# The feed-forward path of a two-layer cross-attention kernel, taken a slot sooner and its first product split around the scores

## What is computed

```python
# layer 0, per batch
qkv  = ln(x, g1, be1) @ w_qkv + b_qkv
ckv  = context @ w_ckv + b_ckv
attn = softmax(mask(q @ concat(k_self, k_ctx).T / sqrt(8)))      # causal over own tokens
x    = x + attn @ concat(v_self, v_ctx)
hdn  = ln(ln(x, g2, be2), gf, bf) @ w1 + b1                      # 128 -> 512
x    = x + gelu(hdn) @ w2 + b2                                   # 512 -> 128
# layer 1, per batch
Q, K, V = ln(x, ln_w, ln_b) @ wq.T + bq, context @ wk.T + bk, context @ wv.T + bv
out  = softmax(key_mask(Q @ K.T / sqrt(8))) @ V @ wo.T + bo + x
```

## Time and profile before

| | |
|---|---|
| median of 3 runs | 465.14 us (463.82 to 467.96) |
| the profiled execution | 466.13 us, its span 463.7 us, mean granted TensorE clock 0.915 |
| PE busy | 384.7 us (83%), 8885 matmuls |
| DVE busy | 295.5 us (64%) |
| ACT busy | 262.5 us (57%) |
| POOL busy | 139.8 us (30%) |
| chain of waits, by engine | PE 50%, DVE 18%, issue 9%, ACT 8%, DMA 8%, POOL 4% |

### The profile page before, as it was taken

The page is one execution under the profiler, slowest core; times in us unless marked ns, Lnnn a source line. Parts: engine busy times, 40 slices in busy tenths (PEclk is TensorE's granted clock), DMA queues, the critical chain, the costliest instruction groups (busy, mean ns, idle before and its releaser), DMA issues.

```text
span 463.7 us, 20194 instructions
## 1 busy us (share of the span) xinstructions
PE 384.7 (83%) x8885; PEld 278.6 (60%) x8885; DVE 295.5 (64%) x738; ACT 262.5 (57%) x459; POOL 139.8 (30%) x207
## 2 busy tenths in 40 slices
PE   3668879996989799988899798979898989686766
PEld 1346657564666576657576567667676676453654
DVE  5426786469568774796658675796389459706232
ACT  2567635763756476464846386556656756343451
POOL 7100533046205520363105520461047106302000
PEclk9957986999999899998999899998999999877586
DMA  6755164115342542153404542253201400121101
GB/s 192 198 151 123 54 171 140 34 56 137 108 119 93 121 147 59 69 129 111 134 3 146 106 131 60 94 122 122 60 26 43 125 3 26 58 82 47 48 4 45
DMA packets 41974, 42.86 MB, mean 92 GB/s; under 512 B 3208, under 2 KB 34392, under 8 KB 41888
## 3 DMA queue, kind: packets, MB, share of 16 engines
q1 hardware_dynamic: 40436, 39.86, 31.2%
q0 software_dynamic: 624, 1.26, 1.0%
q10 hardware_dynamic: 828, 0.46, 0.3%
HBM read 23.65 MB, written 17.83 MB: 89 GB/s over the span
## 4 chain that ended last, share of the span: by engine, by line
PE 50%; DVE 18%; issue 9%; ACT 8%; DMA 8%; POOL 4%; SPq 1%; ACTq 1%; DVEq 0%; POOLq 0%
PE dense L689 12%; PE dense L712 7%; DVE top L1011 5%; PE key L845 3%; PE mixed L875 3%; PE mixed L883 3%; DMA k_stack<-scratch_k 3%; PE key L836 3%; PE side L908 3%; PE dense L694 3%; PE dense L702 2%; PE query L795 2%; PE query L803 2%; DVE k_part L1001 2%; ACT probs L523 2%
## 5 line engine op out<-in xcount | busy, mean ns | idle before, releaser
L1011 DVE TENSOR_REDUCE top<-query 128x8 f32<-128x1024 f32 (+1 forms) x96 | 117.2, 1220 | 70.9 <-PE query L803 54.7
L523 ACT ACTIVATE probs<-key 128x1024 f32<-128x1024 f32 x96 | 98.4, 1025 | 81.9 <-PE key L845 55.7
L462 POOL TENSOR_TENSOR top<-top 128x8 bf16<-128x8 f32 (+1 forms) x96 | 20.3, 213 | 207.2 <-DVE top L1011 206.5
L845 PE MATMUL key<-top_row,spread 48*64 48x128 bf16 x1536 | 48.7, 226 | 3.8 <-ACT top_row L528 3.6
L455 POOL TENSOR_TENSOR rstd_x<-var_eps_x,half 128x4 f32<-128x4 f32 x24 | 24.5, 1020 | 71.6 <-DVE var_eps_x L973 71.6
L544 ACT COPY o_t<-mixed 128x256 f32<-128x256 f32 x96 | 35.3, 368 | 13.4 <-PE mixed L896 7.8
L875 PE MATMUL mixed<-probs,v 128*32 128x128 f32 x1024 | 41.7, 281 | 0.0
L836 PE MATMUL key<-q_stack,k_stack 48*64 48x128 f16 x1024 | 40.1, 221 | 0.0
L689 PE MATMUL dense<-normed_ft,w 128*128 128x512 f32 x64 | 34.2, 663 | 5.1 <-ACT normed_ft L564 5.1
L845 PEld LDWEIGHTS key<-top_row,spread 48*64 48x64 bf16 x1536 | 33.8, 109 | 6.1 <-ACT probs L523 4.9
L908 PE MATMUL side<-cst,o_t 128*128 128x128 f32 x192 | 34.1, 304 | 0.7 <-ACT mix_t L551 0.7
(11 more groups left out here) (120 smaller groups left out, 782.1 us busy)
## 6 DMA issues: line engine op xcount, KB each, us to landing
k_stack<-scratch_k SPq DMA_DIRECT2D x16, 384.0 KB, 6.2
q_stack<-scratch_q SPq DMA_DIRECT2D x64, 96.0 KB
scratch_k<-k_part SPq DMA_DIRECT2D x8, 512.0 KB, 2.8
scratch_k<-k_part SPq DMA_DIRECT2D x16, 256.0 KB, 2.6
scratch_q<-q_part SPq DMA_DIRECT2D x16, 256.0 KB, 2.7
k_stack<-scratch_k SPq DMA_DIRECT2D x16, 192.0 KB
x_in<-in_x SPq DMA_DIRECT2D x8, 256.0 KB, 3.2
scratch_q<-q_part SPq DMA_DIRECT2D x16, 128.0 KB, 2.4
```

The source lines that it names most:

```text
L523: nc.scalar.activation(probs[u.number % 2][:].rearrange("p h q -> p (h q)"), key[:].rearrange("p h x -> p (h x)"), ACT.Exp, scale=SCALE).t ...
L845: ins = nc.tensor.matmul(key[T * n:T * n + T, h, a * P:(a + 1) * P], spread[u.layer][rows, A2 * h + a, T * n:T * n + T], top_row[u.number ...
L1011: nc.vector.tensor_reduce(maxima, query[:].rearrange("p h x -> p (h x)").rearrange("p (a k) -> p a k", a=w), AX_X, ALU.max, negate=True).t ...
```

## The change

The second norm's statistics and root come in slot 10 instead of 11, its rows in slot 11 instead of 12, `f_t` in slot 12 instead of 13. The products with w1 keep their slots (13 and 14), but leave `dense` and `dense_first` for a function of their own, `up`, which PE runs between `by_query` and `by_key`. The GELUs of `w1_0` and `w1_1` stay at the end of ACT's slot 13; those of `w1_2` and `w1_3` are written at the head of slot 14, ahead of the exponential. The one-column GELU is left for the last chunk alone.

```diff
-JOBS = (("f_t", L0, 13), ("w1_0", L0, 13), ...
+JOBS = (("f_t", L0, 12), ("w1_0", L0, 13), ...
...
         @block.gpsimd
-                for c in due(11, s):
+                for c in due(10, s):
                     root(c, "x1_again")
...
         @block.scalar
+            def gelu(c, f):
+                nc.scalar.activation(hidden[:, f, :], job(f"w1_{f}", c)[:], ACT.Gelu,
+                                     bias=cols[:, B1 + f:B1 + f + 1]).then_inc(s_read[f"w1_{f}"], 1)
...
-                for c in job_due("w1_1", s):
+                for c in job_due("w1_0", s):
                     if c > 0:
                         act.wait_ge(s_done["w2b"], c)
-
-                    act.wait_ge(s_half, 1)
-                    nc.scalar.activation(unread[:, c:c + 1], half[:, 0:1], ACT.Gelu)
-                    for f in range(FC):
-                        nc.scalar.activation(hidden[:, f, :], job(f"w1_{f}", c)[:], ACT.Gelu,
-                                             bias=cols[:, B1 + f:B1 + f + 1]).then_inc(s_read[f"w1_{f}"], 1)
+                    if c == LAST:
+
+                        act.wait_ge(s_half, 1)
+                        nc.scalar.activation(unread[:], half[:, 0:1], ACT.Gelu)
+                    gelu(c, 0)
+                    gelu(c, 1)
...
             for s in ALL:
+                for c in job_due("w1_2", s):
+                    gelu(c, 2)
+                    gelu(c, 3)
                 if s + 1 in UNIT:
                     exp(UNIT[s + 1])
...
         @block.tensor
                 for c in job_due("f_t", s):
                     pe.wait_ge(s_norm["x1_again"], c + 1)
                     transposes("f_t", c, normed_f)
+
+            def up(s):
+                for c in job_due("w1_0", s):
+                    pe.wait_ge(s_read["f_t"], c + 1)
+                    product("w1_0", c, w1[:, 0:P], normed_ft)
+                    product("w1_1", c, w1[:, P:2 * P], normed_ft)
                 for c in job_due("w1_2", s):
                     product("w1_2", c, w1[:, 2 * P:3 * P], normed_ft)
                     product("w1_3", c, w1[:, 3 * P:4 * P], normed_ft)
...
-                for c in job_due("w1_0", s):
-                    pe.wait_ge(s_read["f_t"], c + 1)
-                    product("w1_0", c, w1[:, 0:P], normed_ft)
-                    product("w1_1", c, w1[:, P:2 * P], normed_ft)
...
                 if s + 3 in UNIT:
                     by_query(UNIT[s + 3])
+
+                up(s)
                 if s + 1 in UNIT:
                     by_key(UNIT[s + 1])
...
         @block.vector
-                for c in due(12, s):
+                for c in due(11, s):
                     norm_rows(c, "x1_again", normed_f, normed_f)
...
-                for c in due(11, s):
+                for c in due(10, s):
                     dve.wait_ge(s_offset, c + 1)
                     stats("x1_again", normed_f, range(TILES))
```

More of the change, by code:

```diff
@@ L84, in last_unit @@
     return max(u.number for u in UNIT.values() if (u.layer, u.chunk) == (layer, c))
-JOBS = (("f_t", L0, 13), ("w1_0", L0, 13), ("w1_1", L0, 13), ("w1_2", L0, 14), ("w1_3", L0, 14), ("ctx_t", IN, -22),
+JOBS = (("f_t", L0, 12), ("w1_0", L0, 13), ("w1_1", L0, 13), ("w1_2", L0, 14), ("w1_3", L0, 14), ("ctx_t", IN, -22),
         ("w2a", L0, 15), ("k_ctx", IN, -21), ("w2b", L0, 16), ("x_t", IN, -20), ("k0", IN, -19), ("out", L1, 9), ("out_a", OUT_A, 0),
@@ L176, in xattn_program @@
         half = sb("half", [P, TILES])
-        unread = sb("unread", [P, CHUNKS])
+        unread = sb("unread", [P, 1])
         cst = sb("cst", [P, CW])
```

## The result

| | before | the change |
|---|---|---|
| median of 4 runs each | 464.48 us (462.40 to 467.96) | 476.77 us (472.28 to 479.60) |
| ratio, with its interval | | 1.0225 (1.0117 to 1.0332) |
| profiled execution | 466.13 us, span 463.7 us, clock 0.915 | 472.28 us, span 470.4 us, clock 0.918 |
| PE / DVE / ACT busy | 384.7 / 295.5 / 262.5 us | 386.2 / 296.3 / 261.9 us |

The change makes the kernel slower by 12.3 us in the medians; 476.5 was forecast. The ratios in this document are taken over the fast runs alone, without the slow ones (here that of 479.60 us), and so differ a little from the ratio of the medians.

What follows compares the result with a forecast made beforehand. PE, busy 83% of the span and holding half the chain of waits, was taken to bound the kernel. 466.1 + 8.4 (stall less gains) + 3.1 (clock) = 477.6, as a median 476.5; range 468.5 to 483.5.

Steps and rivals of the forecast that it cites:

- The stall: Slot 14, chunks 0 to 6: PE idles 2.44 us ahead of the third product with w1, until the first GELU ends.
- The gains: Per chunk, PE's wait for the scaled `f_t` goes (0.55 us); its wait behind slot 14's exponential shrinks by 0.66.
- The clock in half of the chunks: Behind the idle stretch in slot 14 the clock falls in half of the chunks, 1.26 us each, 4.4 in all.
- rival of a fall in every chunk: The clock falls behind slot 14's idle stretch in all seven chunks: 8.8 us on top of 8.4, 482.3; chance 0.15.
- the one without a fall: Rival: PE's idle stretch in slot 14 costs its 8.4 us and the clock nothing, 473.5; chance 0.2.
- One fall spared: Of four clock falls behind PE's waits without a releaser, chunks 2 to 5, one may go: -1.3 us.
- faster rival: The four waits without a releaser and their falls vanish: at most 15 us back against 8.4, 458.5; chance 0.07.
- The table load: ACT's load ahead of the first GELU costs 1.28 us; with the skill's added drain the stall would be 3.8.
- Chunk 1: PE's wait of 1.22 us ahead of `ctx_t` takes up some 0.3, so this chunk loses 0.9 instead of 1.2.
- Start and tail: Ends of the kernel: only chunk 7 changes, its transposes moving beside ACT's scaling, 0 to 0.5 us, taken as 0.2.
- The distance of the chunks: Sign: first products of chunks 2, 3 and 4 move from 51 us apart to 52.3 or more.
- rival of a loss taken up: A DMA or DVE chain binds behind slot 15 and absorbs half the loss: +4.2, 468.3 as a median; chance 0.1.

Runs made afterwards that it cites:

- half of the change: The change with the third and fourth products with w1 put back behind the scores by key of slot 14; 475.25 us against 462.80, ratio 1.0245.
- the pair of kernels with the stall open and filled: The change, 476.94 us, beside the change with two more overwritten products of 128x512 in PE's idle stretch, 469.56 us; ratios 1.0402 and 1.0217.

## Why the prediction was right

- **The stall** (2.44 predicted): 2.48 or 2.49 in each of chunks 0 to 6, in every profile of the change. The path was to be 12.27 and is 12.40; before 11.05. Shown as cause by three kernels: undoing the first pair's move takes it down to 0.80, half of the change keeps the distance of 6.34, and 0.50 more on ACT makes it 2.99.
- **The gains** (0.55 and 0.66): the first is there. PE does not wait for the scaled `f_t`; alone this brought 5.1 us, with an interval that takes in the 3.9 predicted. The second is only a shift. The wait behind the exponential went from 1.01 to 0.23 (0.35 predicted), but the 5.09 us from the third product to the scores by key of slot 15 are the same before, in the change and with only the first half moved. The prediction subtracts 0.66 there and has the same 0.66 in its 2.44, so the sum of 1.22 per chunk is sound.
- **The clock in half of the chunks** (4.4 us): in five, six and five of seven. Behind the third products 7.6, 8.6 and 8.7 us are lost in the three profiles, 1.4 to 1.7 per fall, of which the pairs have 5.97 in the first. By the pair of kernels with the stall open and filled it is 7.4 us. The mechanism was right and the term too small, by the number of falls and by the price of one: 1.26 counts the pair alone. The upper bound of 2.4 per fall left the pair out; chunk 1 lost 2.52. The rival of a fall in every chunk was nearer to the traces than I gave it chance for, and the one without a fall (473.5) is refuted by them. The rule of the Trainium skill that I weighed (TensorE: Matmul & The Clock Gate, HAM oscillation — how this bites in real kernels) tolerates longer gaps than 2.49 us and does not agree with these traces.
- **One fall spared** (-1.3): two were, in each of the three profiles of the change, and in the first the waits themselves shrank from 10.67 to 7.99. This offset the clock's larger term in part, and it was a part of the faster rival, in small. I had given that rival 0.07.
- **The table load** at 1.28, without the drain of 1380 ns in the Trainium skill (ScalarE: Activation LUTs, What ACT_TABLE_LOAD costs): in chunk 4 the GELU starts at 281.96, 1.30 behind the load's start at 280.66. With a drain the stall would have been 3.8; it is 2.48. The trace does not agree with that page, and the sum was right not to use it.
- **Chunk 1** was to lose 0.3 less, because PE waits there for its context anyway. That wait of 1.22 is gone in the profile of the change, as forecast.
- **Start and tail** were taken as unchanged but for 0.2. The stretch from chunk 7's first product on is 2.8, 2.8 and 1.2 us shorter in the three profiles of the change than in the profile before. Part of it is the clock in its eight products, which take 4.76, 4.79 and 5.69 us instead of 6.39; the rest was not followed.
- **The distance of the chunks** was to grow from 51 us to 52.3 or more. In the first profile it is 51.71 and 53.68, so the sign holds for both, the size only for their sum; from chunk 4's to chunk 5's the distance fell, from 49.91 to 48.80, where the wait without a releaser is 0.59 instead of 2.04.
- **A slip** in the rival of a loss taken up: 466.1 + 4.2 - 1.0 is 469.3 and not 468.3. So that case lies inside the range of 468.5 to 483.5 and not at its lower end; the outcome does not hang on it.

The median of 476.77 agrees with 476.5 better than the terms do: a path and a clock term that were larger than forecast, and shorter waits with fewer falls behind them, cancelled. The direction and the path were worked out; that the number is right to 0.3 us is luck. In two later sets of runs, on two different chips, the change stood 2.8% and 4.0% above the kernel before, with intervals from 1.0222 to 1.0333 and from 1.035 to 1.0454, so its loss varies between such sets more than within one; of what, no run here tells.

## What to carry to other kernels

When two jobs share two buffers with the next two, ask what the reader of the first buffer still has to do when the writer comes back: moving a product ahead of the work that feeds the reader delays the reader by that product and the writer by the whole of the reader's run. Moving the third product alone was free; moving the first put a stall of 2.5 us into every round. A wait that gets shorter is a gain only if the path through it gets shorter: the 1.01 us that became 0.23 brought nothing, because the next step waited for ScalarE either way. And an idle stretch of PE on the critical path has two prices, itself and the clock behind it: count both, and test the second by filling the stretch with work that nobody reads.

## What the runs showed of the hardware

- Idle stretches of PE of 2.48 or 2.49 us, between busy ones, were followed by a lengthened pair of products in 16 of 21 cases over three profiles; one of 1.58 in 1 of 7; of 0.80 and 0.57 in none. Of ten waits without a releaser of 1.92 to 3.01 us in the same three profiles, six were followed by a fall and four (1.92, 2.14, 2.24, 2.96) were not, so among these the length does not decide.
- An ACT_TABLE_LOAD stood behind the wait of the activation that needs it (idle of 0.24 at 219.01 and of 0.68 at 219.95 ahead of the load, for the product that the GELU reads). With a one-column activation in front the load starts at once (220.03, with the exponential over at 220.01), and the GELU follows 1.40 behind the load's start.
- Filling an idle 2.49 us with two products of 128x512 that nobody reads made the kernel 7.4 us faster in the medians.
